# Attention and sparse feed-forward on one core: weight operands made on DVE once and stored, P1 seeded into P2's bank, steps of the attention part reordered

## The chip, the cores and the metric

The kernel runs on one NeuronCore of a Trainium2 chip. The metric is device time of one execution in microseconds (us), lower is better. The engines are TensorE (PE, with PEld for its weight loads), VectorE (DVE), ScalarE (ACT), GpSimd (POOL) and SyncE (SP), which here only issues DMAs.

## The reference

The input x is 2048 x 512. It is layer-normalised, xn = layernorm(x), and the result is x + attention(xn) + ffn(xn):

```
x_norm = layernorm(xn) * gamma + beta
q, k, v = x_norm @ qkv            # 512 x 512 each, one head, causal
attention = softmax(q k^T / sqrt(512)) v @ o_proj + xn
h = silu(xn @ w_gate) * (xn @ w_up)          # 2048 wide
ffn = keep_2_of_4(h) @ w_down                # of every 4, the 2 largest in magnitude
```

Everything is float32.

## The kernel before, in words

**Precision.** Each float32 operand is split into a part rounded to fp32r (hi) and the rest (lo), and each product is three matmuls: hi hi, hi lo, lo hi. ACT makes the hi parts (a cast), and DVE or POOL the lo parts (a subtraction). The three matmuls are lines 511 to 513 in attention, 635 to 637 for gate and up, 712 to 714 for down.

**Attention** (lines 66 to 102, 114 to 126, and the loops over `steps`). The 2048 rows are 4 chunks of 512, or 16 tiles of 128. q and k are folded into one matrix (mu), v and o_proj into another (vo). For each chunk there are statistics (`stat`, `x_stats`, `x_rstd`, `x_scale`), a way of turning them into rows (`row_turn`, `row_store`, `row_spread`; for chunk 0 `x_rows` and `x_turn`), xh (the normalised, transposed x: `xh_pre` on DVE, an affine step and the hi part on ACT, the lo part on DVE), `z` (mu times xh) and `v` (one product for each tile), and `xn`, the transposed layernorm of x, which is stored to DRAM (`xn_store`) for the feed-forward part. For each tile i there are `scores`, `exp`, `head` (PE turns the first two groups of 4 key tiles), and `attend` (the other turns and the products with v). The order is written out by hand in the list `steps`: what stands in `before`, `between` and `beside` is put in front of head i, behind it, and between scores i+1 and attend i. Every engine runs the same list in order and does its own part of each step, with semaphores between the engines, so an engine that waits in one step holds back all that it has in later ones. PE's products share 4 banks, its turns 3.

In the kernel before, POOL does these steps: `x_rstd`, the lo part of the last weight splits (line 479), `xn` (lines 487 and 490), and the weight sums and lo parts (lines 446 to 456).

**Feed-forward** (from line 630). The rows are worked in two passes of 1024, and each pass in 8 sets of 256 hidden units for each of the 4 positions in a group of 4; N_Q = 16 sets, n = 0 to 15. Gate and up of a set are each a 2 x 2 block product, done with 7 products by Strassen's scheme in Winograd's form: P1 to P7, on operands A11, A12, A22 and the sums S1 to S4 of the weights, and B11, B21, B22 and T1 to T4 of x. `block_product` is 6 matmuls, so a set has 14 x 6 = 84. PE's order is P1, P2, P6, P7, P5, P3, P4, gate and up in turn, in banks 0 and 1 (X), 2 and 3 (Y), 4 and 5 (Z). P1, P1+P6, P1+P6+P5 grow in X; ACT copies each stage to SBUF (`snapshot`, line 827). P2 is made in Y by itself, and DVE adds the copy of P1 to it (`add_sum` with fill F_P2); P7 and P4 are in Z and DVE adds copies to them (`add_sum`, line 1066). ACT applies silu, DVE multiplies by up (`hidden`, line 1072).

Then the 2 of 4 are picked for half a set, i = n - 2: ACT makes magnitudes (line 831), DVE compares them (`first_beats`, `last_beats`), counts (`count_beats`), zeroes (`keep`), ACT and DVE split the result (`kept_hi`, `kept_lo`), and PE multiplies by w_down (`down`: 48 matmuls in 4 tiles that alternate between banks 6 and 7; a tile needs the bank that `add_down`, line 1082, of two tiles ago set free). PE's order is gate_up(n), down(n-2), gate_up(n+1).

The waits that matter here: P4 of gate waits for the sum of P7 (`summed`), as it is added to the same bank; P2 waits only for DVE's sum of the set before; P6 waits for the copy of P1.

For each of the 16 sets, 1 MB of weights is loaded (`load_set`), POOL makes S1 to S4 (lines 446 to 451, in two halves), ACT the hi parts (line 745, 4 x 896 columns) and POOL the lo parts (line 455), though the second pass uses the same weights. There are two operand buffers, `wset[0]` and `wset[1]`. The down weights of two halves (1 MB) are loaded, split by ACT (`down_hi`) and POOL (`down_lo`) for every second set. Between the passes, X's operands are made again for the other 1024 rows (`X_first` to `X_fourth`, `X_lo_half` on DVE, `X_halves` on ACT); they are seven pairs of hi and lo.

Of the kernel before, what the change touches and what calls it, by code (L numbers as in the profile page):

```python
# [26 lines left out]
def attention_ffn(nc, x, x_t, qkv_t, o_proj, gamma, beta, w_units, w_down, out):  # L27
# [45 lines left out]
    between = {3: [z[1][1], row_turn[2], row_store[2], *z[1][2:4], row_spread[2]],  # L73
               7: z[2],
               11: z[3]}
    beside = {0: [v[0][1], *stat[2][2:4], x_stats[2], x_rstd[2], xt_load[2]],
              1: [xh_pre[1][0], v[0][2], xh_pre[1][1]],
              2: [*xh[1], v[0][3], x_scale[2], xn_store[0]],
              3: [*xn[1], stat[3][0], stat[3][1]],
              4: [v[1][0], stat[3][2], stat[3][3], x_stats[3], x_rstd[3], xt_load[3]],  # L80
              5: [v[1][1], *xh_pre[2], x_scale[3], xn_store[1]],
              6: [v[1][2], row_turn[3], row_store[3], *xh[2], row_spread[3]],
              7: [v[1][3], *xn[2]],
              8: [xn_store[2], v[2][0]],
              9: [v[2][1], *xh_pre[3]],
              10: [v[2][2], *xh[3], *xn[3]],
              11: [v[2][3], xn_store[3]],
              12: [*v[3], ("w_load", 0, 0)],
              13: [("w_sum", 0, 0), ("w_sum", 0, 1), ("w_hi", 0, 0), ("w_hi", 0, 1), ("w_lo", 0, 0), ("w_lo", 0, 1)],
              14: [("w_hi", 0, 2), ("w_hi", 0, 3), ("w_lo", 0, 2), ("w_lo", 0, 3)]}  # L90
# [38 lines left out]
    with ExitStack() as ctx:  # L129
# [36 lines left out]
        beats_a, beats_b = at("beats_a", 56 * KB, [P, 2, W], BF16), at("beats_b", 58 * KB, [P, 2, W], BF16)  # L166
        beats_c, pair_sum = at("beats_c", 60 * KB, [P, 2, W], BF16), at("pair_sum", 62 * KB, [P, 2, W], BF16)
# [4 lines left out]
        wsum_early = [at(f"wsum_early{m}", o * KB, [P, 2, NOP, P], F32) for m, o in enumerate((56, 168))]  # L172
        acc = at("acc", 96 * KB, [P, 2 * TC, D], F32)
        dw = at("dw", 112 * KB, [P, 2, 2, 2, D], F32R)
        dw_last = at("dw_last", 0, [P, 2, 2, 2, D], F32R)
        dw_raw, dw_last_raw = at("dw_raw", 112 * KB, [P, 2, 2, 2, D], F32), at("dw_last_raw", 0, [P, 2, 2, 2, D], F32)
        g_sum = [at(f"g_sum{i}", (160 + 2 * i) * KB, [P, W], F32) for i in range(4)]
# [4 lines left out]
        last_mag = [at(f"last_mag{i}", o * KB, [P, G, W], F32) for i, o in enumerate((128, 64))]  # L182
        last_hi = [at(f"last_hi{i}", (o + 8) * KB, [P, G, W], F32R) for i, o in enumerate((128, 64))]
        last_lo = [[at(f"last_lo{i}_{r}", (o + 16 + 2 * r) * KB, [P, W], F32R) for r in range(G)] for i, o in enumerate((128, 64))]
# [1062 lines left out]
```

## Time and profile before

| | |
|---|---|
| median of 3 runs | 963.36 us (962.62 to 967.53) |
| the profiled execution | 965.22 us |
| its span, first to last instruction | 963.4 us |
| instructions | 9777 |
| mean granted clock of TensorE | 0.940 of full speed |
| PE busy | 850.4 us (88%) |
| DVE busy | 637.4 us (66%) |
| ACT busy | 342.1 us (36%) |
| POOL busy | 350.0 us (36%) |
| DMA | 66.72 MB, mean 69 GB/s |

Matmul rows overlap: one shows 0.39 us from start to end at full clock, though the next starts 0.23 us after it. The lists of groups and of single instructions name an engine, a line, and tiles as out<-in. "Idle before" is how long the engine had stood still, and behind the arrow what ended it. Times in the trace count from the first instruction; attention ends and the first feed-forward set begins at 374.0, set 2 at 412.1, set 15 at 900.3.

### The profile page before, as it was taken

Reading aid. Unit: us, or ns where it says so; the run is one execution under the profiler, and the core shown is the slowest. Engines: PE = TensorE matmul, PEld = TensorE weight load, DVE = VectorE, ACT = ScalarE, POOL = GpSimd, SP = SyncE. Lnnn points to the kernel's source line nnn. Section 1 sums busy time; section 2 is a strip of 40 time slices with the busy share of each in tenths; the row PEclk is TensorE's granted clock in tenths of the full one; section 3 lists DMA queues with packets and bytes.
Section 4 is the critical chain, followed back from the end, with each engine's and each line's share of the span. In section 5 each row is a group of like instructions: output and inputs, shape, how many; then the busy total and the mean of one; then the engine's idle time right before and its main releaser. Section 6 shows DMA issues by size and latency. Waiting matters only on the chain. (4 is left out here: it accounts for less than half of the span.)

```text
span 963.4 us, 9777 instructions
## 1 busy us (share of the span) xinstructions
PE 850.4 (88%) x3635; PEld 690.3 (72%) x3635; DVE 637.4 (66%) x919; ACT 342.1 (36%) x546; POOL 350.0 (36%) x259
## 2 busy tenths in 40 slices
PE   7796898989999998988898898887898988988987
PEld 5575776777778887867686686676776776866875
DVE  6846474235323346396966966999769769669597
ACT  5413214113212325443443443454434334434341
POOL 2324031003002232674464455455625724734120
PEclk9987999999999999998898998897988988998999
DMA  9323233001001132211011021221034020120102
GB/s 339 119 76 111 77 110 121 22 22 66 23 23 55 33 142 97 100 44 45 25 64 44 3 85 44 88 88 55 33 113 150 1 87 13 32 72 17 45 0 88
DMA packets 32319, 66.72 MB, mean 69 GB/s; under 512 B 3168, under 2 KB 3216, under 8 KB 31888
## 3 DMA queue, kind: packets, MB, share of 16 engines
q1 hardware_dynamic: 28096, 58.50, 18.1%
q10 hardware_dynamic: 4176, 7.60, 2.3%
q8 instruction: 29, 0.48, 0.2%
q14 instruction: 18, 0.15, 0.1%
HBM read 53.48 MB, written 12.61 MB: 69 GB/s over the span
## 5 line engine op out<-in xcount | busy, mean ns | idle before, releaser
L635 PE MATMUL bank<-X_hi,wset 128*128 128x512 f32 x448 | 189.4, 423 | 62.8 <-DVE g_sum L1066 58.9
L455 POOL TENSOR_TENSOR wset<-wsum,wset 128x896 fp32r<-128x896 f32 x60 | 140.5, 2368 | 175.3 <-ACT wset L745 175.3
L636 PE MATMUL bank<-X_lo,wset 128*128 128x512 f32 x448 | 186.0, 415 | 0.0
L637 PE MATMUL bank<-X_hi,wset 128*128 128x512 f32 x448 | 185.7, 415 | 0.0
L635 PEld LDWEIGHTS bank<-X_hi,wset 128*128 128x128 f32 x448 | 91.3, 204 | 88.4 <-DVE g_sum L1066 59.8
L637 PEld LDWEIGHTS bank<-X_hi,wset 128*128 128x128 f32 x448 | 91.1, 203 | 20.3
L636 PEld LDWEIGHTS bank<-X_lo,wset 128*128 128x128 f32 x448 | 91.9, 205 | 19.1
L1082 DVE TENSOR_TENSOR acc<-bank,acc 128x512 f32<-128x512 f32 x64 | 43.4, 689 | 83.8 <-PE bank L714 83.8
L712 PE MATMUL bank<-dw,hs_hi 128*128 128x512 f32 x224 | 88.4, 395 | 0.0
L713 PE MATMUL bank<-dw,hs_hi 128*128 128x512 f32 x224 | 87.8, 392 | 0.0
L714 PE MATMUL bank<-dw,hs_lo 128*128 128x512 f32 x224 | 87.3, 390 | 0.0
L446 POOL TENSOR_TENSOR wsum<-wsum 128x256 f32<-128x256 f32 x30 | 24.0, 801 | 163.6 <-DMA wsum<-w_units 163.6
L511 PE MATMUL bank<-v_hi,pT_hi 128*128 128x512 f32 x136 | 55.6, 409 | 11.0 <-issue 7.4
L511 PE MATMUL bank<-xT_hi,zg_hi 128*128 128x512 f32 (+3 forms) x160 | 59.2, 370 | 5.6 <-DVE zg_lo L1011 5.6
L513 PE MATMUL bank<-xT_hi,zg_lo 128*128 128x512 f32 (+3 forms) x160 | 58.1, 363 | 0.0
L512 PE MATMUL bank<-xT_lo,zg_hi 128*128 128x512 f32 (+3 forms) x160 | 58.0, 362 | 0.0
L1023 DVE TENSOR_SCALAR_CACHE_REDUCE raw<-bank 128x512 f32<-128x512 f32 (+3 forms) x36 | 21.5, 600 | 54.0 <-PE bank L513 54.0
L745 ACT CAST wset<-wsum 128x896 fp32r<-128x896 f32 x60 | 53.3, 938 | 4.5 <-POOL wsum L451 4.5
L513 PE MATMUL bank<-v_hi,pT_lo 128*128 128x512 f32 x136 | 53.8, 395 | 0.0
L512 PE MATMUL bank<-v_lo,pT_hi 128*128 128x512 f32 x136 | 53.6, 394 | 0.0
L487 POOL TENSOR_TENSOR xt_raw<-xt_raw,spread 128x1024 f32<-128x1024 f32 x8 | 19.5, 2434 | 90.7 <-DVE xh_raw L993 90.7
L739 ACT CAST pT_hi<-bank 128x512 fp32r<-128x512 f32 (+3 forms) x40 | 19.6, 524 | 87.2 <-PE bank L553 42.9
(164 smaller groups left out, 1755.2 us busy)
## 6 DMA issues: line engine op xcount, KB each, us to landing
wsum<-w_units SPq DMA_DIRECT2D x60, 256.0 KB, 3.7
dw_raw<-L_ffn_w_down SPq DMA_DIRECT2D x14, 512.0 KB, 4.7
xw<-L_attn_x SPq DMA_DIRECT2D x4, 1024.0 KB, 9.3
xt_raw<-x_t SPq DMA_DIRECT2D x8, 512.0 KB, 7.0
xn_t<-xt_raw SPq DMA_DIRECT2D x8, 512.0 KB, 7.4
X_raw<-xn_t SPq DMA_DIRECT2D x8, 512.0 KB, 4.2
acc<-resid SPq DMA_DIRECT2D x2, 2048.0 KB, 9.3
result<-acc SPq DMA_DIRECT2D x16, 256.0 KB, 2.3
```

What stands on the lines that cost most here:

```text
L455: nc.gpsimd.tensor_tensor(wset[q % 2][:, m, 1, :, :], sums_at(q, m), wset[q % 2][:, m, 0, :, :].bitcast(F32), ALU.subtract).then_inc(w_op_ ...
L511: pe.matmul(dst, l_hi, r_hi, start=(n == 0 and flags.get("first", True)), stop=False)
L512: pe.matmul(dst, l_hi, r_lo, start=False, stop=False)
L513: last = pe.matmul(dst, l_lo, r_hi, start=False, stop=(n == len(pairs) - 1 and flags.get("last", True)))
L635: pe.matmul(dst[:], u[:, 0, :], x_hi, start=(first and kt == 0), stop=False, skip_group_check=True)
L636: pe.matmul(dst[:], u[:, 0, :], x_lo, start=False, stop=False, skip_group_check=True)
L637: last = pe.matmul(dst[:], u[:, 1, :], x_hi, start=False, stop=(kt == 1), skip_group_check=True)
L712: pe.matmul(dst, s_hi, d_h, start=(r == 0), stop=False)
L713: pe.matmul(dst, s_hi, d_l, start=False, stop=False)
L714: last = pe.matmul(dst, s_lo, d_h, start=False, stop=(r == G - 1))
L745: nc.scalar.copy(wset[q % 2][:, m, 0, :, :], sums_at(q, m)).then_inc(w_hi, 1)
L1082: nc.vector.tensor_tensor(acc[:, tile, :], down_bank(i, t)[:], acc[:, tile, :], ALU.add).then_inc(added, 1)
```

## The change

It does these things:

- The sums, the lo parts of the weight operands, the lo parts of the down weights, the last lo parts of the v/o splits and xn are issued on DVE. POOL keeps only `x_rstd` and the constants. The sums are one group of four operations of 512 columns for each set, where they were two groups of 256.
- The operands of sets 0 to 7 are stored to a DRAM tensor as they are made (3.67 MB each, `store_set`), and sets 8 to 15 load them from there (`load_made`), with no sums, hi or lo parts.
- ACT copies P1 from banks 0 and 1 to banks 2 and 3, and P2 is accumulated on top of it; ACT applies silu to bank 2 itself, and DVE multiplies by bank 3 (`first_hidden`). The two DVE adds of P1 to P2 go. P2 waits for the copies.
- Each v product is a tile ahead of where it was, and v of a new chunk stands behind its z. The rows of chunk 0 are turned ahead of the first two v/o weight products. xn, xh and statistics steps stand at other tiles.
- In tile 15 ACT makes two X halves ahead of its probabilities, not four, and DVE makes the X sums behind them.
- Some buffers have other places; the last down weights are loaded a little later.

```diff
+    wop_dram = nc.dram_tensor("w_operands", (NQ, P, 4 * 2 * NOP * P), F32, kind="Internal").ap()
...
-              xw_load[2], xt_load[1], split[2][2], split[3][2], split[2][3], split[3][3], x_scale[0], ("x_rows", 0, 0), vo[0], vo[1],
-              ("x_turn", 0, 0), *xh_pre[0], vo[2], xh[0][0], stat[1][0], xh[0][1], stat[1][1], vo[3], xh[0][2], stat[1][2], xh[0][3],
-              stat[1][3], x_stats[1], x_rstd[1], *xn[0], xw_load[3], *z[0][0:2], x_scale[1], z[0][2], row_turn[1], row_store[1], z[0][3],
-              ("scores", 0, 0), row_spread[1], exp[0], v[0][0], *stat[2][0:2]]
+              xw_load[2], xt_load[1], split[2][2], split[3][2], x_scale[0], ("x_rows", 0, 0), split[2][3], split[3][3],
+              ("x_turn", 0, 0), vo[0], vo[1], *xh_pre[0], vo[2], xh[0][0], stat[1][0], xh[0][1], stat[1][1], vo[3], xh[0][2], stat[1][2],
+              xh[0][3], stat[1][3], x_stats[1], x_rstd[1], xw_load[3], *z[0][0:2], x_scale[1], z[0][2], row_turn[1], row_store[1],
+              z[0][3], row_spread[1], ("scores", 0, 0), exp[0], v[0][0], xn[0][0], v[0][1], xn[0][1], xn_store[0]]
     before = {3: [z[1][0]]}
...
+    between = {3: [z[1][1], x_scale[2], *z[1][2:4], v[1][0]],
+               7: [*z[2], v[2][0]],
+               11: [*z[3], v[3][0]]}
+    beside = {0: [v[0][2], xh_pre[1][0]],
+              1: [xh_pre[1][1], v[0][3], *xh[1][0:2]],
+              2: [*xh[1][2:4], *stat[2], x_stats[2], x_rstd[2], xt_load[2]],
+              3: [v[1][1], *stat[3], x_stats[3], x_rstd[3], xt_load[3]],
+              4: [v[1][2], row_turn[2], row_store[2], *xn[1], row_spread[2], xn_store[1], x_scale[3]],
+              5: [v[1][3], *xh_pre[2]],
+              6: [row_turn[3], row_store[3], *xh[2], row_spread[3], *xn[2], xn_store[2]],
+              8: [v[2][1]],
+              9: [v[2][2], *xh_pre[3]],
+              10: [v[2][3], *xh[3], *xn[3], xn_store[3]],
+              11: [v[3][1]],
+              12: [*v[3][2:4], ("w_load", 0, 0)],
+              13: [("w_sum", 0, 0), *fills("w_hi", 0)],
+              14: fills("w_lo", 0)}
...
+            def flat(q):
+                return wset[q % 2][:].bitcast(F32).rearrange("p m h o i -> p (m h o i)")
+            def store_set(q):
+                sp.wait_ge(w_op_ready, 4 * q + 4)
+                sp.dma_start(wop_dram[q], flat(q)).then_inc(set_stored[q % 2], 16)
+            def load_made(n):
+                q = n % NQ
+                sp.wait_ge(set_stored[q % 2], 16 * (q // 2 + 1))
+                sp.dma_start(flat(n), wop_dram[q]).then_inc(set_loaded[n % 2], 16)
...
                 if n + 2 < N_Q:
                     sp.wait_ge(full[1], FILLS * (n + 1))
-                    load_set(n + 2)
+                    if n + 2 < NQ:
+                        sp.wait_ge(set_stored[n % 2], 16 * (n // 2 + 1))
+                        load_set(n + 2)
+                    else:
+                        load_made(n + 2)
+                if n + 1 < NQ:
+                    store_set(n + 1)
...
                 X_wait(1)
                 for m in range(2):
-                    if n:
-                        pe.wait_ge(summed[m], 3 * (n - 1) + 1)
-                    block_product(m, n, A12, B21, Y[m], True)
+                    pe.wait_ge(kept[m], 3 * n + 1)
+                    block_product(m, n, A12, B21, Y[m], False)
...
-                snapshot(0, n, F_P1, bank[0], g_sum[0], 4 * (n - 1) + 1 if n else 0, 0)
-                snapshot(1, n, F_P1, bank[1], a_tile(n, 0), 0, a_free(n))
-                act.wait_ge(summed[0], 3 * n + 1)
-                nc.scalar.activation(g_sum[0][:], g_sum[0][:], ACT.Silu).then_inc(silu_ready, 1)
+                snapshot(0, n, F_P1, bank[0], bank[2], 4 * (n - 1) + 1 if n else 0, 0)
+                snapshot(1, n, F_P1, bank[1], bank[3], 0, 0)
+                act.wait_ge(full[0], FILLS * n + F_P2)
+                nc.scalar.activation(g_sum[0][:], bank[2][:], ACT.Silu).then_inc(silu_ready, 1)
+                early = n == 0 or 3 <= n < NQ - 1
+                if early:
                     operands_hi(n + 1, 0)
                     operands_hi(n + 1, 1)
...
+                if early or n == 1:
+                    for m in range(2 if early else 0, 4):
+                        operands_hi(n + 1, m)
+                if n >= 4 and n % 2 == 0:
                     down_hi(n // 2 - 1)
+                elif n == N_Q - 1:
+                    down_hi(ND // 2 - 1)
...
+                if n == 1:
+                    down_hi(0)
+                elif n == 2:
+                    for m in range(4):
+                        operands_hi(n + 1, m)
...
                     if n == NT - 1:
-                        for i in range(NOP):
+                        X_first(0)
+                        X_second(0)
+                        X_third(0)
+                        X_fourth(0)
+                        dve.wait_ge(X_summed, 4)
+                        for i in range(4):
+                            X_lo_half(0, i)
+                        sums(1)
+                        for i in range(4, NOP):
                             X_lo_half(0, i)
...
                 if picks:
                     first_beats(i)
-                add_sum(0, n, bank[2], F_P2, g_sum[0], 1)
-                add_sum(1, n, bank[3], F_P2, a_tile(n, 0), 1)
-                if picks:
                     last_beats(i)
-                hidden(n, 1, 1, g_sum[0], a_tile(n, 0))
+                first_hidden(n)
                 if picks:
                     count_beats(i)
                     keep(i, 0)
                     keep(i, 1)
+                if n == 0:
+                    operands_lo(1, 0)
+                    operands_lo(1, 1)
+                elif n <= 2:
+                    sums(n + 1)
+                if n == 1:
+                    for m in range(4):
+                        operands_lo(2, m)
+                if n >= 4 and n % 2 == 0:
+                    down_lo(n // 2 - 1)
+                elif n == N_Q - 1:
+                    down_lo(ND // 2 - 1)
                 add_sum(0, n, bank[4], F_P7, g_sum[2], 3)
...
+                elif picks and n < NQ - 1:
+                    operands_lo(n + 1, 0)
+                    operands_lo(n + 1, 1)
+                    add_down(i, 0)
+                    operands_lo(n + 1, 2)
+                    operands_lo(n + 1, 3)
+                    add_down(i, 1)
+                    add_down(i, 2)
+                    if n + 2 < NQ:
+                        sums(n + 2)
+                    add_down(i, 3)
```

## Rows read from the trace of the kernel before

**Rows 1.** The page, busy tenths of POOL in 40 equal slices of the span.
```profile
POOL 2324031003002232674464455455625724734120
```

**Rows 2.** PE's waits: line waited for, us in total, times, longest.
```profile
PE bank L635 <- DVE g_sum L1066: 58.9, 13, 7.1
PE bank L635 <- ACT g_sum L827: 3.9, 2, 3.5
PE bank L712 <- issue: 2.7, 1, 2.7
PE bank L712 <- DVE last_lo L1117: 2.6, 3, 2.2
...
PE bank L511 <- issue: 15.2, 5, 7.8
PE bank L553 <- issue: 5.8, 4, 1.4
PE bank L511 <- DVE zg_lo L1011: 5.6, 4, 1.4
...
PE bank L543 <- DVE row_stat L976: 4.9, 1, 4.9
PE bank L511 <- DVE pT_lo L916: 3.7, 3, 3.0
```

**Rows 3.** Stretches: length, busy PE, PEld, DVE, ACT, POOL (x), PEclk, DMA share, GB/s.
```profile
45.00:105.00 60.00, 46.55 (x192) 37.22 (x193) 33.49 (x72) 14.46 (x29) 20.09 (x13) 0.83 0.27 92
...
374.00:412.10 38.10, 38.10 (x170) 31.56 (x169) 16.25 (x21) 19.54 (x29) 23.81 (x16) 1.00 0.34 118
412.10:900.30 488.20, 425.44 (x1718) 344.58 (x1717) 384.21 (x441) 196.14 (x308) 243.40 (x171) 0.91 0.17 54
```

**Rows 4.** Timeline of set 6, from 563.06: start us, length us, engine, line.
```profile
563.26 2.20 ACT L831 ACTIVATE mag<-hid_a 128x512 f32<-128x512 f32 x4 [8.58 <-PE bank L714]
565.36 0.56 ACT L827 COPY g_sum<-bank 128x512 f32<-128x512 f32 x1
...
570.03 5.08 POOL L455 TENSOR_TENSOR wset<-wsum,wset 128x896 fp32r<-128x896 f32 x2 [8.04 <-ACT wset L745]
...
570.51 2.62 DVE L1072 TENSOR_TENSOR hid_a<-g_sum,hid_a 128x512 f32<-128x512 f32 x1
573.05 2.61 DVE L1098 TENSOR_TENSOR pair_sum<-beats_b,beats_c 128x1024 bf16<-128x1024 bf16 x1
...
583.43 0.68 DVE L1066 TENSOR_TENSOR g_sum<-bank,g_sum 128x512 f32<-128x512 f32 x1
...
584.17 0.80 PE L635 MATMUL bank<-X_hi,wset 128*128 128x512 f32 x1 [4.62 <-DVE g_sum L1066]
```

**Rows 5.** Timeline of DVE in set 15, with POOL idle.
```profile
908.33 0.69 DVE L1098 TENSOR_TENSOR pair_sum<-beats_b,beats_c 128x1024 bf16<-128x1024 bf16 x1
909.05 0.42 DVE L1100 TENSOR_TENSOR beats_b<-beats_b,beats_c 128x512 bf16<-128x512 bf16 x1
```

**Rows 6.** Groups by form: busy us, mean ns of one, idle before.
```profile
L745 ACT CAST wset<-wsum 128x896 fp32r<-128x896 f32 x60 | 53.3, 938 | 4.5 <-POOL wsum L451 4.5
...
L1087 DVE TENSOR_TENSOR beats_a<-mag 128x1024 bf16<-128x1024 f32 x14 | 17.1, 1224 | 19.6 <-ACT mag L831 19.6
```

**Rows 7.** Timeline in attention: row scale, splits of chunk 1, a turn, a split.
```profile
42.55 2.30 DVE L969 SCALAR_TENSOR_TENSOR row_stat<-mean_var,row_stat 128x4 f32<-128x4 f32 x1 [1.41 <-POOL rstd L476]
...
81.34 6.54 DVE L1002 TENSOR_TENSOR xT_lo<-xh_raw,xT_hi 128x512 fp32r<-128x512 f32 x4 [2.24 <-ACT xT_hi L781]
...
236.47 0.52 PE L553 MATMUL bank<-ident,raw 128*128 128x128 f32 x3 [1.45 <-issue]
...
241.16 0.69 DVE L1002 TENSOR_TENSOR xT_lo<-xh_raw,xT_hi 128x512 fp32r<-128x512 f32 x1 [0.68 <-ACT xT_hi L781]
```

**Rows 8.** DMA: a stretch with a full queue (columns as rows 3), and an issue.
```profile
10.00:28.00 18.00, 17.23 (x80) 13.91 (x79) 15.36 (x31) 7.67 (x14) 6.04 (x8) 1.00 1.06 387
...
xw<-L_attn_x SPq DMA_DIRECT2D x4, 1024.0 KB, 9.3
```

More of the change, by code:

```diff
@@ L180, in attention_ffn @@
         hs_lo = [at(f"hs_lo{r}", o * KB, [P, W], F32R) for r, o in enumerate((156, 158, 92, 94))]
-        last_mag = [at(f"last_mag{i}", o * KB, [P, G, W], F32) for i, o in enumerate((128, 64))]
-        last_hi = [at(f"last_hi{i}", (o + 8) * KB, [P, G, W], F32R) for i, o in enumerate((128, 64))]
-        last_lo = [[at(f"last_lo{i}_{r}", (o + 16 + 2 * r) * KB, [P, W], F32R) for r in range(G)] for i, o in enumerate((128, 64))]
+        last_at = ((0, 8, 32), (64, 72, 80))
+        last_mag = [at(f"last_mag{i}", o[0] * KB, [P, G, W], F32) for i, o in enumerate(last_at)]
+        last_hi = [at(f"last_hi{i}", o[1] * KB, [P, G, W], F32R) for i, o in enumerate(last_at)]
+        last_lo = [[at(f"last_lo{i}_{r}", (o[2] + 2 * r) * KB, [P, W], F32R) for r in range(G)] for i, o in enumerate(last_at)]
         hid_a = [at(f"hid_a{i}", (176 + 2 * i) * KB, [P, W], F32) for i in range(6)]
@@ L689, in bank_free @@
                 elif i == ND - 3:
-                    pe.wait_ge(summed[t - 2], 3 * last + 1)
+                    if t == 2:
+                        pe.wait_ge(silu_ready, 4 * last + 1)
+                    else:
+                        pe.wait_ge(hid_ready, 4 * last + 1)
                 elif i == ND - 2:
@@ L696, in bank_free @@
                     else:
-                        pe.wait_ge(summed[t - 2], 3 * last + 3)
+                        pe.wait_ge(summed[t - 2], 2 * last + 2)
                 else:
@@ L806, in _ @@
                     if n == NT - 1:
-                        X_halves(0, range(4))
+                        X_halves(0, range(2))
                 elif kind == "attend":
@@ L949, in _ @@
             for kind, n, k in steps:
-                if kind == "split" and not pool_splits(n, k):
+                if kind == "split":
                     dve.wait_ge(w_hi_ready[n], k + 1)
@@ L993, in _ @@
                     nc.vector.tensor_tensor(part, part, row_over(n, 3), ALU.add).then_inc(xh_scaled, 1)
+                elif kind == "xn":
+                    t = xt_raw[n][k]
+                    if n == 0:
+                        dve.wait_ge(rows_kept, 2)
+                    done = step(nc.vector.tensor_tensor(t[:], t[:], row_over(n, 0), ALU.mult))
+                    dve.wait_ge(vec_step, done)
+                    nc.vector.tensor_tensor(t[:], t[:], row_over(n, 1), ALU.add).then_inc(xn_ready[n], 1)
+                elif kind == "w_sum":
+                    sums(n)
+                elif kind == "w_lo":
+                    operands_lo(n, k)
                 elif kind == "row_turn":
@@ L1066, in add_sum, with first_hidden @@
                 nc.vector.tensor_tensor(dst[:], src[:], dst[:], ALU.add).then_inc(summed[m], 1)
+            def first_hidden(n):
+                dve.wait_ge(silu_ready, 4 * n + 1)
+                dve.wait_ge(full[1], FILLS * n + F_P2)
+                if a_free(n):
+                    dve.wait_ge(hs_ready, a_free(n))
+                nc.vector.tensor_tensor(a_tile(n, 0)[:], g_sum[0][:], bank[3][:], ALU.mult).then_inc(hid_ready, 1)
             def hidden(n, result, sums, silu, up):
@@ L1070, in hidden @@
                 if sums:
-                    dve.wait_ge(summed[1], 3 * n + sums)
+                    dve.wait_ge(summed[1], 2 * n + sums)
                 nc.vector.tensor_tensor(up[:], silu[:], up[:], ALU.mult).then_inc(hid_ready, 1)
@@ L1123, in last_block @@
                 add_sum(1, n, bank[5], F_P4, a_tile(n, 1), 3)
-                hidden(n, 4, 3, g_sum[1], a_tile(n, 1))
+                hidden(n, 4, 2, g_sum[1], a_tile(n, 1))
             for n in range(N_Q):
@@ L1146, in _ @@
                     kept_lo(i, 1)
-                hidden(n, 2, 2, g_sum[2], b_tile(n, 1))
+                hidden(n, 2, 1, g_sum[2], b_tile(n, 1))
                 if picks:
@@ L1159, in _ @@
                     last_block(n)
+                if n == 1:
+                    down_lo(0)
                 if n == NQ - 1:
```

161 lines of the change are left out of this document (51 added, 110 removed).

## The prediction

> **What bounds the kernel now.** I read the busy tenths first: TensorE (PE) is the busiest engine, and POOL is at work a third of the time and more from attention's end on [rows 1]. Then who holds PE up: 58.9 us go to one wait, 13 times, on the vector engine's sum in line 1066 [rows 2]. Then the stretches. Sets 0 and 1 of the feed-forward part take 38.1 us for 168 matmuls with no stall and clock 1.00, so a matmul is worth 0.2268 us and a full set (84 gate/up and 48 down matmuls) 29.9 us; yet the 13 sets from 412.1 to 900.3 take 488.2 us where 13 x 29.9 = 389 would do, at clock 0.91 [rows 3]. Of these 99 us, 62 are PE's waits for sums and copies [rows 2]; the other 37, 2.8 a set, are matmuls at the lower clock level (1.2 GHz) after each wait: the first one after it takes 0.80 us [rows 4].
>
> The timeline of set 6 says why the sum is late. DVE's product of silu and up, its pair sum and its counts take 2.5 to 2.6 us each, and run side by side with four POOL operations of that same length; the sum of P7 then starts at 583.43, and PE, which needed it for P4 at 579.5, has lost 4.6 us [rows 4]. At 908 to 909, with POOL idle, the same operations take 0.69 and 0.42 us [rows 5]. So a POOL operation with operands in SBUF holds back a DVE operation with two SBUF inputs for its whole length; those that read PSUM stay at 0.68 [rows 4]. In attention it is the same: 2.30 us for a 4-column operation at 42.55, in front of PE's 4.9 us wait, and 6.54 us for four splits at 81.34, in front of PE's 7.8 us wait [rows 2, 7].
>
> **Feed-forward, the part that goes.** All large POOL work goes. In a set DVE loses one product at 2.62 to 0.69, a pair sum at 2.61 to 0.69 and two counts at 2.5 to 0.42: 8 us, and two g_sum adds of 0.68 (P2 now adds itself). Counted from the set's start, DVE then has keep 0 and 1 behind it at about 11, while the copy of P5 it also needs comes at 13.2; in even sets the two down_lo (1.2 each by the 1024-column row [rows 6]) end at 14.2. P7's sum is done at 14.8 at the latest and PE wants it at 16.5. The wait goes in all 13 sets, and with it the lower clock: 99 us.
>
> **What it adds.** (a) P2 starts only when P1 was copied. ACT comes to that copy behind four magnitudes, 2.20 us, and needs 0.56 [rows 4]: ready at 2.9 of the set, against PE at 2.72. The trace has no copy from PSUM to PSUM. From below it is the copy from PSUM to SBUF, 0.56 [rows 4], from above twice that. I take the row, whose source and size are the same: 0.2 us in each of 13 sets, 2.6; at double length it would be 0.9 a set, 9 more in all. The Trainium skill (ScalarE: Activation LUTs, Step-by-step: what each stage is for) says ScalarE writes PSUM sooner than SBUF; by that the sum would lose at most the 2.6; no row here shows such a write.
> (b) Operands on DVE, sets 2 to 6: sums 4 x 0.69 = 2.7; four lo of 896 columns between 0.69 (512) and 1.22 (1024), 1.09 each and 1.04 apart: 4.2. A set's other DVE work, at its undisturbed pace, is two comparisons of 1024 columns at 1.14, the counts with the pair sum at 3.0, and 22 operations of 512 columns that follow one another every 0.6: 18.5, so it has 25.4, or 27.8 in even sets, of 29.9. Two lo stand in front of add_down 0, which frees the bank for PE's third down tile: DVE is through at 25.1, PE wants it at 24.7. 0.45 in four sets, 1.0 in set 2, where ACT makes the hi halves last: 2.8.
> (c) Set 8: without POOL the second X pass is faster on DVE (X_lo 1.2 each), but P2 now waits for ACT, whose four last X halves (1.05 each) run to 32.2 from set 7's start, then magnitudes and the copy: 34.9 against 32.8. 2.1 us, and DVE a bit late behind it: 2.3.
> (d) Second pass: DVE and ACT have no operand work. What must arrive is one 3.67 MB load a set, issued when a gate/up ends and needed 41 us later. With the queue full the engines move 387 GB/s [rows 8]: 9.5 us, hidden. Stores of 3.67 MB in the first pass stand before the next down weights in the same queue: issued at 27.6 of set 3 they end at 8 of set 4, the weights land at 10 and 11.5, ACT comes for them at 10.8. Nothing, but with 0.3 us to spare; at half that rate the store ends 9 later and it is up to 9 us in sets 4 and 6 each.
> (e) The end: last_mag's first comparison no longer sits beside POOL, and down_hi is off ACT's path there: PE's wait of 2.7 and its clock go, the 2.2 us wait on last_lo stays [rows 2]: 63.1 becomes 58.8.
> (f) SP's waits: in the first pass it waits for the store of a buffer's last set before it loads the next one (stored nearly a set before), then for DVE's last lo of the following set (27.6) before it stores that; behind it stand only the down weights, which wait for down's end at 30.5 anyway, and, in sets 8 and 9, result stores with the second pass's acc load behind them: that load is issued at some 33 of set 9 and used at 22 of set 10. Moved buffers cost nothing, except that dw_last may be loaded only when set 14's products are done, 19 us into it, for ACT at 9 of set 15. In set 1 the sums of set 2 wait for its load; in the trace its second half is summed 6.7 us after the set's start, where DVE now comes for it at 6.5: 0.2 us, before a P7 sum with 2 us of room.
> Sum: 38.2 + 389 + 2.6 + 2.8 + 2.3 + 58.8 = 493.7 us, for 589.4 now.
>
> **Attention, 374 us now.** SP's row store and spread for chunks 2 and 3 stay ahead of the xn stores and of the xh steps that need them by a tile. Up to 105: the x_scale in front of the row turn shrinks to 0.5, -3.9; z of chunk 1 waits 5.9 instead of 8.2 (xn's four DVE steps of 1.25 delay tile 2 by 2.5, the splits come sooner), -2.3; the 1.4 wait of scores behind z goes, since v stands between, -1.4. The clock there, 0.83 over 60 us [rows 3], is 20 us at the lower level, some 6 of them idle, so it costs 7; I leave 2, -5. The rows' turn now stands before the first v/o weight products, and PE idles from 19.4 to 23.1: +3.6. Together -9.
> From 105 on: seven waits of 1.45 (the one at 236.47 stands for them) [rows 2, 7] and one of 3.0 for the split of a just made v go, as v is a tile ahead: -13.2; two waits behind z, -2.8; the wait of 3.0 in tile 15 goes, ACT has two X halves there and not four, with its clock -4.7 [rows 2].
> New are waits for in-order work. Tile 10: v, then four ACT/DVE splits 1.38 apart, end 9.5 us after the scores (241.16 + 0.69), as now; two xn of 2.5 follow on DVE and only then pT_lo of the third key group: 15.1, where PE wants it at 8.5: +6.6, and 2.5 of clock. Tile 13: sums on DVE, then four hi parts of 0.94 on ACT [rows 6] before its pT_hi: +3.2. Tile 7: v no longer covers chunk 2's splits, z waits 2.5. Tiles 9 and 14: 1.1. Together +15.9.
> 374 - 9 - 20.7 + 15.9 = 360.2.
>
> **The sum.** 360.2 + 493.7 = 853.9 of span; the profiled execution was 1.8 us over its span (965.2), so 855.7, and it stood 1.9 above the median of the runs (963.4). Forecast: 854 us, against 963.4.
>
> **The rivals.**
> The copy from PSUM to PSUM is long, or ACT comes late to it, so that PE stalls at every P2: 16 x 0.9, 868. For it: no row shows such a copy. Chance 0.10.
> Attention gives back what it gains (xn and sums stand in DVE's order in front of pT_lo in more tiles than I traced): 374, so 868. 0.07.
> DVE is the bound of the first pass. Against: 2 us of slack in each set by the steps above. For: the order is fixed, and one late load of weights (d) goes into the next set. Then sets 2 to 7 keep a wait like now, 4.4 and 2.8 us of clock: +43, 897. 0.10.
> The edit removes no stall, because the 2.6 us rows were slow by themselves: then DVE gets 7 us a set more and it ends near 975. The 0.42 us rows of the same shapes speak against it [rows 5]. 0.01.
> Slower than before: the SP queue becomes the bound. It now carries 3.67 + 1 + 0.5 MB in each first-pass set and 3.67 + 0.5 MB in each second-pass set, 75 MB in place of some 25; the sets wait when that takes longer than they do. At 387 GB/s it is 194 us of 494. The 1 MB xw loads took 9.3 us from issue to landing [rows 8], 113 GB/s: at that rate 75 MB need 664 us, and the kernel about 1025. It decides below 128 GB/s (75 MB in the 589 us of now). 0.03.
> A measurement of this kernel can tell about 0.5%, 5 us, from no change. The forecast has the rest, 0.69.
>
> **The numbers.** The forecast's own range is 836 to 880 (clock fully back and no new wait in attention at the low end, 16 below; the 9 us of (a) and the 18 of (d) at the high end). It takes in the first two rivals; for 8 in 10 the range reaches to most of the DVE case: 836 to 892. Faster by over 0.5%: 0.69 + 0.10 + 0.07 + 0.10 less a little for mishaps not named = 0.95. Within: 0.01. Slower: 0.04.
>
> **What would show it.** PE's wait on line 1066's successor is gone or under 5 us in total, DVE has no row over 1.3 us for 512 columns, and the mean clock is near 0.98. The sets from 2 to 14 are 30 to 31 us apart. P2 starts 0.1 to 0.3 us after P1 ends. In tile 10 PE waits some 6 us for pT_lo, at 19.4 some 3.7 us for the rows. The 3.67 MB loads and stores take 9 to 12 us each. It is wrong if PE waits at P4 in the first pass, if it waits at a set's start in the second (the load), or if DVE's long rows stay with POOL idle.

## The result and the profile after

The changed kernel takes 877.5 us (median of 4 runs, 875.8 to 878.3) against 963.0 before (962.5 to 967.5): ratio 0.910, 95% interval 0.907 to 0.913. That is inside the predicted range, on the predicted side, and 23 us above the point forecast of 854. The profiled execution took 875.8 us with a span of 874.0.

The page says that PE's busy share rose from 88% to 94%, and POOL's busy time fell from 350.0 us to 13.7.

```profile
PE 825.3 (94%) x3635; PEld 672.0 (77%) x3635; DVE 578.8 (66%) x985; ACT 314.1 (36%) x514; POOL 13.7 (2%) x33
...
PEclk9898999999899999999999999999999999999998
```

PE's waits. The first line of [rows 2], 58.9 us for the sum of P7, has no successor at all; nothing waits at P4 any more. What remains is spread over many small ones, most of them in attention.

```profile
PE bank L473 <- DVE pT_lo L887: 12.6, 5, 6.3
PE bank L473 <- issue: 6.0, 2, 3.3
PE bank L473 <- DVE xT_lo L946: 5.5, 1, 5.5
PE bank L597 <- DVE X_lo L919: 4.4, 1, 4.4
PE bank L548 <- DVE rows_wide L974: 4.0, 1, 4.0
PE bank L597 <- ACT bank L794: 3.7, 2, 1.9
PE bank L679 <- DVE last_lo L1132: 3.3, 4, 2.7
```

The stretches, with the columns of [rows 3]: attention in three parts, sets 0 and 1, sets 2 to 14, and the end.

```profile
0.00:45.00 45.00, 33.49 (x131) 27.06 (x132) 29.58 (x57) 21.59 (x35) 5.23 (x17) 0.92 0.62 222
45.00:105.00 60.00, 52.19 (x229) 41.28 (x227) 34.42 (x80) 16.87 (x33) 5.33 (x11) 0.91 0.27 93
105.00:369.20 264.20, 246.31 (x1167) 204.11 (x1166) 125.13 (x263) 64.51 (x104) 3.14 (x6) 0.98 0.22 78
...
369.20:410.20 41.00, 40.98 (x169) 33.52 (x170) 29.72 (x37) 22.04 (x33) 0.00 (x0) 0.94 0.52 199
410.20:812.40 402.20, 397.23 (x1717) 322.85 (x1716) 310.01 (x469) 167.80 (x276) 0.00 (x0) 0.99 0.46 175
...
812.40:874.00 61.60, 55.08 (x229) 43.13 (x228) 49.90 (x80) 21.31 (x36) 0.00 (x0) 0.96 0.09 35
```

The 13 sets from 2 to 14 took 488.2 us at clock 0.91; they now take 402.2 at 0.99. The first feed-forward matmul starts at 369.2, where it started at 374.0. So the feed-forward part gave 84.6 us of span and attention 4.8.

The timeline of set 6 (from 536.3): ACT's two copies of P1, and DVE. It answers to [rows 4].

```profile
538.62 1.19 ACT L794 COPY bank<-bank 128x512 f32<-128x512 f32 x2
...
542.37 0.69 DVE L1081 TENSOR_TENSOR hid_a<-g_sum,bank 128x512 f32<-128x512 f32 x1
542.97 0.68 DVE L1113 TENSOR_TENSOR pair_sum<-beats_b,beats_c 128x1024 bf16<-128x1024 bf16 x1
543.69 0.42 DVE L1115 TENSOR_TENSOR beats_b<-beats_b,beats_c 128x512 bf16<-128x512 bf16 x1
...
548.28 2.36 DVE L910 TENSOR_TENSOR dw<-dw_raw,dw 128x1024 fp32r<-128x1024 f32 x2 [1.03 <-ACT dw L717]
550.55 0.68 DVE L1073 TENSOR_TENSOR g_sum<-bank,g_sum 128x512 f32<-128x512 f32 x1
```

The pair sum and the counts have the durations that they had beside an idle POOL in [rows 5], and the product of silu and up, which now reads a bank, takes 0.69 us. P7's sum starts 14.2 us after the set's start, where it was 20.4; PE wants it at 16.5.

The DMA issues that are new took what was expected, and no set waits for one:

```profile
w_operands<-wset SPq DMA_DIRECT2D x8, 3584.0 KB, 12.0
wset<-w_operands SPq DMA_DIRECT2D x8, 3584.0 KB, 11.6
```

Two waits in the profile have a cause that the prediction did not name. The first is behind DVE's order in tile 15:

```profile
356.87 0.69 DVE L887 TENSOR_TENSOR pT_lo<-bank,pT_hi 128x512 fp32r<-128x512 f32 x1 [3.12 <-ACT pT_hi L706]
360.08 0.69 DVE L887 TENSOR_TENSOR pT_lo<-bank,pT_hi 128x512 fp32r<-128x512 f32 x1 [2.52 <-ACT pT_hi L706]
361.88 0.55 DVE L1051 TENSOR_SCALAR rows<-rows,one_rstd,neg_mean_rstd 128x512 f32<-128x512 f32 x1 [1.10 <-DMA rows<-L_attn_x]
362.34 2.55 DVE L914 TENSOR_TENSOR X_raw<-X_raw,X_raw 128x1024 f32<-128x1024 f32 x2
365.34 2.36 DVE L914 TENSOR_TENSOR X_raw<-X_raw,X_raw 128x1024 f32<-128x1024 f32 x2 [0.46 <-DVE X_raw L914]
367.74 4.63 DVE L919 TENSOR_TENSOR X_lo<-X_raw,X_hi 128x1024 fp32r<-128x1024 f32 x4
```

DVE stands idle for 3.1 and 2.5 us between the turned groups, then waits for the last row tile, and only then makes the X sums: PE stands for 4.4 us ahead of set 0. The second is ACT at the start of set 2, with the matmul that waits for it:

```profile
410.16 1.99 ACT L717 CAST dw<-dw_raw 128x1024 fp32r<-128x1024 f32 x2
412.05 2.19 ACT L798 ACTIVATE mag<-hid_a 128x512 f32<-128x512 f32 x4
414.14 1.05 ACT L794 COPY bank<-bank 128x512 f32<-128x512 f32 x2
...
414.77 0.50 PE L597 MATMUL bank<-X_hi,wset 128*128 128x512 f32 x1 [1.83 <-ACT bank L794]
```

### The profile page after: what moved, and what is told of

It reads as the page before. It is cut to its first block and busy times, and to the rows that moved or that the text cites. A ratio compares the mean times of both kernels' runs of the same rounds, so it can differ in the third digit from the quotient of the medians.

```text
span 874.0 us, 9524 instructions
## 1 busy us (share of the span) xinstructions
PE 825.3 (94%) x3635; PEld 672.0 (77%) x3635; DVE 578.8 (66%) x985; ACT 314.1 (36%) x514; POOL 13.7 (2%) x33
## 5 line engine op out<-in xcount | busy, mean ns | idle before, releaser
L597 PE MATMUL bank<-X_hi,wset 128*128 128x512 f32 x448 | 178.5, 398 | 8.7 <-DVE X_lo L919 4.4
L599 PE MATMUL bank<-X_hi,wset 128*128 128x512 f32 x448 | 176.6, 394 | 0.0
L598 PE MATMUL bank<-X_lo,wset 128*128 128x512 f32 x448 | 176.6, 394 | 0.0
L597 PEld LDWEIGHTS bank<-X_hi,wset 128*128 128x128 f32 x448 | 85.5, 191 | 32.8 <-ACT bank L794 7.9
L599 PEld LDWEIGHTS bank<-X_hi,wset 128*128 128x128 f32 x448 | 85.4, 191 | 18.2
L598 PEld LDWEIGHTS bank<-X_lo,wset 128*128 128x128 f32 x448 | 85.6, 191 | 17.4
L473 PE MATMUL bank<-xT_hi,zg_hi 128*128 128x512 f32 (+3 forms) x160 | 58.9, 368 | 1.4 <-DVE zg_lo L1016 1.4
L679 PEld LDWEIGHTS bank<-dw,hs_hi 128*128 128x128 f32 x224 | 42.0, 188 | 11.5 <-DVE acc L1097 2.9
L681 PEld LDWEIGHTS bank<-dw,hs_lo 128*128 128x128 f32 x224 | 42.1, 188 | 8.8
L680 PEld LDWEIGHTS bank<-dw,hs_hi 128*128 128x128 f32 x224 | 42.0, 188 | 8.5
L473 PEld LDWEIGHTS bank<-v_hi,pT_hi 128*128 128x128 f32 x136 | 26.4, 194 | 21.1 <-DVE pT_lo L887 12.0
## 6 DMA issues: line engine op xcount, KB each, us to landing
wset<-w_operands SPq DMA_DIRECT2D x8, 3584.0 KB, 11.6
```

What stands on the lines that cost most here:

```text
L473: pe.matmul(dst, l_hi, r_hi, start=(n == 0 and flags.get("first", True)), stop=False)
L597: pe.matmul(dst[:], u[:, 0, :], x_hi, start=(first and kt == 0), stop=False, skip_group_check=True)
L598: pe.matmul(dst[:], u[:, 0, :], x_lo, start=False, stop=False, skip_group_check=True)
L599: last = pe.matmul(dst[:], u[:, 1, :], x_hi, start=False, stop=(kt == 1), skip_group_check=True)
L679: pe.matmul(dst, s_hi, d_h, start=(r == 0), stop=False)
L680: pe.matmul(dst, s_hi, d_l, start=False, stop=False)
```

## The experiments

Two questions: which part of the change gave the 85 us, and where the 23 us are that the forecast had and the run did not.

**Seed alone, on the kernel before.** POOL keeps its work.

```diff
-                snapshot(0, n, F_P1, bank[0], g_sum[0], ...)
-                snapshot(1, n, F_P1, bank[1], a_tile(n, 0), ...)
+                snapshot(0, n, F_P1, bank[0], bank[2], ...)
+                snapshot(1, n, F_P1, bank[1], bank[3], 0, 0)
...
-                    block_product(m, n, A12, B21, Y[m], True)
+                    block_product(m, n, A12, B21, Y[m], False)
...
-                add_sum(0, n, bank[2], F_P2, g_sum[0], 1)
-                add_sum(1, n, bank[3], F_P2, a_tile(n, 0), 1)
...
-                hidden(n, 1, 1, g_sum[0], a_tile(n, 0))
+                first_hidden(n)
```

> The kernel before, with P1 copied into P2's bank by ACT and the two adds of P1 to P2 gone; POOL keeps all its work. Contention theory (the gain is the end of POOL's work beside DVE's): the long DVE rows stay at 2.5 to 2.6 us, DVE is only 2 x 0.68 = 1.4 us a set earlier, so each of the 13 waits at P4 shrinks from about 4.5 to about 3.1 and the 2.8 us of lower clock behind it stays; a wait of 0.3 to 0.5 us at P2 is new. 963 - 13 x 1.4 + 5 = 950 us (942 to 958). Rival (the seed takes P1's sum out of the chain and that frees the sets): the waits at P4 fall under 1 us and the time to 880 or less.

927.1 us (ratio to before 0.962, 0.960 to 0.964), between what the theory and the rival gave. The timeline of DVE in its set 5 (from 515.9) shows what the expectation had missed:

```profile
521.98 0.69 DVE L1075 TENSOR_TENSOR hid_a<-g_sum,bank 128x512 f32<-128x512 f32 x1
522.59 2.16 DVE L1107 TENSOR_TENSOR pair_sum<-beats_b,beats_c 128x1024 bf16<-128x1024 bf16 x1
524.78 2.24 DVE L1109 TENSOR_TENSOR beats_b<-beats_b,beats_c 128x512 bf16<-128x512 bf16 x1
526.94 2.33 DVE L1110 TENSOR_TENSOR beats_b<-beats_b,beats_c 128x512 bf16<-128x512 bf16 x1
529.31 2.23 DVE L1112 TENSOR_TENSOR pair_sum<-pair_sum,beats_a 128x512 bf16<-128x512 bf16 x1
531.46 0.41 DVE L1113 TENSOR_TENSOR pair_sum<-pair_sum,beats_a 128x512 bf16<-128x512 bf16 x1
```

Four rows of DVE are still held to 2.2 us beside four POOL lo parts, so contention is there, as expected. But with P1 seeded, the product of silu and up reads a PSUM bank and not two SBUF tiles, and it takes 0.69 us while POOL works. So the seed spares DVE the two adds and a little of the hold as well. P7's sum starts 17.9 us after the set's start, where in set 5 of the kernel before it was 19.8: 1.4 us of these 2.0 are the adds, and 0.6 is the hold, since a count takes the place of the product beside POOL and four rows are still held. Outside sets 2 and 8, PE stands still at P4 for 1.8 to 2.7 us, where it was 4.1 to 4.6 before. And behind waits that short the lower clock came only in some sets: over sets 2 to 14 the clock is 0.97, for 0.91 before, and that is the larger part of what the expectation missed. The row of sets 2 to 14, and the stretches of gate and up in set 3 and in set 5 of this run, where waits of 1.77 and 1.76 us show both cases (clock 0.93 and 1.00):

```profile
410.00:860.00 450.00, 410.61 (x1717) 326.93 (x1716) 363.80 (x415) 197.24 (x308) 241.96 (x170) 0.97 0.18 59
...
447.50:470.50 23.00, 21.18 (x85) 16.73 (x84) 21.13 (x24) 13.01 (x21) 11.81 (x8) 0.93 0.00 0
...
515.90:537.40 21.50, 19.69 (x86) 15.63 (x86) 19.57 (x21) 12.47 (x21) 11.64 (x8) 1.00 0.00 0
```

**The seed taken out of the changed kernel** (the reverse of the edit above).

> The changed kernel without the seed: P2 made by itself, and DVE adds the copies of P1 to it again. Contention theory: DVE has 1.4 us a set more to do, in front of the sum of P7, which had about 2 us to spare; so no wait over 1.5 us comes at P4, and the waits at P2 (0.34 a set, 1.8 in set 2, 1.9 in set 8) go. 872 to 880 us. Rival (the seed carries the gain): 3 to 5 us at P4 and the lower clock return in each set from 2 to 14, 940 us or more.

874.9 us (0.907, 0.904 to 0.909): within what the contention theory gave, and a little under the changed kernel. Two waits are at P4, 0.6 us in set 2 and 2.5 in set 8, where none over 1.5 was expected; in the eleven other sets from 2 to 14 there is none. With P2 by itself the second-pass sets are 29.92 us apart, exactly 132 matmuls at full clock; with the seed they are 30.26. In a kernel without POOL's work the seed brings nothing that shows. The four times together:

| | POOL's work on POOL | on DVE, stored for pass 2 |
|---|---|---|
| P2 alone, two adds | 963 | 875 |
| P2 on a seed of P1 | 927 | 877.5 |

(the right column also has the changed attention part, worth about 5, which no run has by itself). The two gains don't add: both shorten the same DVE chain ahead of P7's sum, and in the changed kernel that sum already starts 2.3 us before PE wants it (14.2 for 16.5).

**No store: the second pass makes its operands again, on DVE.**

```diff
-                    if n + 2 < NQ:
-                        sp.wait_ge(set_stored[n % 2], 16 * (n // 2 + 1))
-                        load_set(n + 2)
-                    else:
-                        load_made(n + 2)
-                if n + 1 < NQ:
-                    store_set(n + 1)
+                    load_set(n + 2)
...
-                early = n == 0 or 3 <= n < NQ - 1
+                early = n == 0 or 3 <= n < N_Q - 1
```

(with `operands_lo` and `sums` issued on DVE in sets 7 to 14 as in 3 to 6)

> The changed kernel without stores and loads of made operands: DVE and ACT make sums, hi and lo parts in the second pass too, as in sets 3 to 7; no w_operands traffic. If contention with POOL was all, DVE has room for them: sets 9 to 14 are 30.7 us apart as sets 3 to 7 are, where they were 30.3, and set 8 starts a few us later as two sets' operand work meets the X work in set 7: 882 us (879 to 892). Rival (what counts is that the second pass has less work): the waits at P4 return in the second pass, 7 x 7.2 = 50 us, 925 or more.

881.1 us (0.914, 0.912 to 0.915). Sets 9 to 14 are 30.7 us apart, 0.43 more each, and sets 7 and 8 take 7.3 us more together; sets 0 to 2 are 2.9 shorter and the end 1.3, with less lower clock there. The longest wait at P4 is 1.3 us. In the sets that the edit touches, storing 29 MB and loading it again is worth some 10 us (7.3 and 6 x 0.43); the difference between the two times is 3.6, as less lower clock in other stretches gives back 4 in this run, by no mechanism that was found.

**A dose of POOL work in the second pass**, which nothing waits for.

```diff
+            for n in range(9, 14):
+                pool.wait_ge(full[0], FILLS * n + F_P1)
+                for _ in range(8):
+                    if n in (9, 10):
+                        small_step(nc.gpsimd.tensor_tensor(scratch[:], X_hi[6][:, 0, :].bitcast(F32), X_hi[6][:, 1, :].bitcast(F32), ALU.add))
+                    elif n == 12:
+                        small_step(nc.gpsimd.tensor_copy(scratch[:], X_hi[6][:, 0, :].bitcast(F32)))
+                    else:
+                        small_step(nc.gpsimd.memset(scratch[:], 0.0))
```

> The changed kernel, with eight POOL operations of 128x512 f32 on a scratch tile added in each of sets 9 to 13, from the end of P1: in sets 9 and 10 an add with two SBUF inputs, in 11 and 13 a memset, in 12 a copy with one SBUF input. Nothing waits for them. Contention theory: beside the adds, DVE's product of silu and up, its pair sum and counts are stretched to the length of a POOL add (over 1.2 us, from 0.69 and 0.42), the sum of P7 comes 4 to 6 us later and PE waits 2 to 4 us at P4 in sets 9 and 10, with the lower clock behind it: +8 to +14 us. If only operand reads hold DVE, sets 11 and 13 are as in the changed kernel; if writes do too, they wait as well. Rival (DVE's long rows had to do with its own work): no DVE row grows, 877 us.

885.6 us (one run), and a wait of 1.8 us at P4 in set 9 (2 to 4 was expected) and of 4.1 in set 10; none in 11, 12 and 13. POOL's timeline in sets 10, 11 and 12, and under it one form of DVE (a comparison of two SBUF tiles, 128x512) in the same three sets, and in set 10 the product that reads a bank:

```profile
665.84 13.72 POOL L474 TENSOR_TENSOR scratch<-X_hi 128x512 f32<-128x512 f32 x8 [18.91 <-PE bank L610]
703.19 4.61 POOL L478 MEMSET scratch<- 128x512 f32 x8 [23.63 <-PE bank L610]
733.82 8.45 POOL L476 COPY scratch<-X_hi 128x512 f32<-128x512 f32 x8 [26.03 <-PE bank L610]
...
670.37 1.77 DVE L1118 TENSOR_TENSOR beats_c<-mag 128x512 bf16<-128x512 f32 x1
706.25 0.69 DVE L1118 TENSOR_TENSOR beats_c<-mag 128x512 bf16<-128x512 f32 x1
736.99 1.09 DVE L1118 TENSOR_TENSOR beats_c<-mag 128x512 bf16<-128x512 f32 x1
...
673.76 0.67 DVE L1092 TENSOR_TENSOR hid_a<-g_sum,bank 128x512 f32<-128x512 f32 x1
```

A POOL add lasts 13.72 / 8 = 1.72 us and the DVE row beside it 1.77; a POOL copy lasts 1.06 and DVE's row 1.09; beside memsets of 0.58 the row stays at 0.69. So in these rows a DVE operation with two SBUF inputs lasts as long as the POOL operation beside it if that one reads SBUF, be it one tile or two, and is not held by one that only writes. The rest of set 10 is held less evenly: the pair sum takes 1.18 us there and three counts 1.40 to 1.51, for 0.69 and 0.42 beside an idle POOL. The product of g_sum with a PSUM bank isn't held: 0.67 beside the adds. The Trainium skill (SBUF — State Buffer, Who interferes with whom) describes just this, a lock for the whole instruction between GpSimd operations that read SBUF and DVE operations with two SBUF inputs; the runs agree, with these numbers.

**The weight work back on POOL in the first pass** (sets 2 to 7; stores, seed and second pass unchanged).

```diff
+            for q in range(2, NQ):
+                pool.wait_ge(w_op_ready, 4 * q)
+                sums(q)
+                for m in range(4):
+                    operands_lo(q, m)
```

(`sums` and `operands_lo` on POOL, taken out of DVE's loop)

> The changed kernel, with the sums and lo parts of the weights of sets 2 to 7 back on POOL (stores, seed and second pass unchanged). Contention theory: sets 3 to 7 look as in the run with the seed alone, with DVE rows of 2.2 us or more and 2 to 3 us waits at P4: 2 to 4.5 us more for each, less 0.4 of down waits that go, so +8 to +18 us in sets 2 to 7, and sets 9 to 14 stay 30.26 us apart: 885 to 895 us. Rival (operand work on DVE is a load that POOL would spare it): sets 3 to 7 become 0.4 us faster, 875 us.

894.5 us (one run), 17 more. Waits at P4 of 4.6, 4.0, 1.8 and 4.0 us are back in sets 3 to 6, with DVE rows of 2.1 to 2.3 us, and sets 9 to 14 stay 30.26 us apart. The time is as expected, though three of the four waits are longer than the 2 to 3 us that were written down, and set 7, in which no operands are made, has none.

Then the missing 23 us.

**X sums in DVE's idle time.**

```diff
                 elif kind == "attend":
+                    if n == NT - 1:
+                        X_first(0)
+                        X_second(0)
                     for g in groups_of(kind, n):
                         probs_lo(n, g)
+                        if n == NT - 1 and g == HEAD:
+                            X_third(0)
+                            X_fourth(0)
+                    if n == NT - 1:
+                        X_lo_half(0, 0)
+                        X_lo_half(0, 1)
                     dve.wait_ge(rows_loaded[slot], 16 * (n // 2 + 1))
...
-                        X_first(0)
-                        X_second(0)
-                        X_third(0)
-                        X_fourth(0)
```

> The changed kernel, with tile 15's X sums and the first two X lo parts issued on DVE in its idle time between the last turns, ahead of the scale of the last rows (whose load lands at 361.9). If their place was the cause, PE's wait of 4.4 us before set 0 and the 2.7 us of lower clock behind it go: 871 us (869 to 874). Rival (X's loads are late themselves, or ACT's X halves are): the wait stays above 2 us, and the time within 3 us of the changed kernel's.

866.9 us (0.900, 0.897 to 0.902), 2 under the expected range. The X sums now run at 354.2 and 358.1:

```profile
354.22 2.54 DVE L914 TENSOR_TENSOR X_raw<-X_raw,X_raw 128x1024 f32<-128x1024 f32 x2
357.47 0.69 DVE L887 TENSOR_TENSOR pT_lo<-bank,pT_hi 128x512 fp32r<-128x512 f32 x1 [0.70 <-ACT pT_hi L706]
358.07 2.35 DVE L914 TENSOR_TENSOR X_raw<-X_raw,X_raw 128x1024 f32<-128x1024 f32 x2
```

PE's wait ahead of set 0 is gone, set 0 starts 4.0 us earlier and sets 0 to 2 are 2.7 us shorter. The edit accounts for 6.7 us. Another 1.0 is in sets 3 to 14, where no lower clock followed set 8's wait in this run (its row there has clock 1.00, for 0.92 in the changed kernel), and 0.8 in the end; the last 2 of the 10.6 stand in the medians and not in the two profiled executions.

**P1's copies ahead of magnitudes.**

```diff
+                    mags_first = 0 if n in (2, NQ) else 2
                     for r in range(G):
+                        if r == mags_first:
+                            snapshot(0, n, F_P1, bank[0], bank[2], 4 * (n - 1) + 1, 0)
+                            if not r:
+                                snapshot(1, n, F_P1, bank[1], bank[3], 0, 0)
                         ...
                         magnitude(i, r)
```

> The changed kernel, with ACT's copy of P1 of gate put between the second and third magnitude, and in sets 2 and 8 both copies ahead of all four. P2's waits go: 13 x 0.34 = 4.4 us, and in sets 2 and 8 2.0 of wait and 1.6 of clock each: 877 - 11 = 866 us (864 to 871; the upper end because in sets 2 and 8 the comparisons start 2 to 3 us later on DVE and P7's sum may be late by 1 to 2 us). Rival (DVE is so full in the first pass that the later magnitudes come back as a wait at P4 in even sets): 872 or more.

870.7 us (0.903, 0.900 to 0.905), at the upper end of what was expected. All waits at P2 are gone and ordinary sets are 0.34 us shorter, but in sets 2 and 8 P7's sum now comes 0.8 and 2.2 us late, as the comparisons start later on DVE, and down of set 2 waits 1.6 us: set 8 gains nothing.

**xn of chunk 3 behind head 11.**

```diff
-               11: [*z[3], v[3][0]]}
+               11: [*xn[3], xn_store[3], *z[3], v[3][0]]}
...
-              10: [v[2][3], *xh[3], *xn[3], xn_store[3]],
+              10: [v[2][3], *xh[3]],
```

> The changed kernel, with xn of chunk 3 moved on DVE from tile 10, ahead of its third turned group, to behind head 11, beside chunk 3's z products. Tile 10's wait of 6.3 us becomes 1 to 2 (the four splits of xh remain) and the lower clock behind it 0 to 1: 870 us (868 to 873). Rival (in-order work only moves): z's lo parts come late behind the 5 us of xn and PE waits 3 us or more in tile 11 or 12: 875 or more.

868.6 us (0.901, 0.898 to 0.903). Tile 10's wait falls from 6.3 to 1.55 us, its lower clock goes, and nothing waits in tiles 11 and 12: z's 48 matmuls cover the 5 us of xn.

**All of it, and more moves of the same kind.**

The further moves: two xh splits of chunks 1, 2 and 3 go behind heads 2, 6 and 10, the sums and hi parts of set 0 go from tile 13 to ahead of head 14, and `add_down` goes ahead of the lo parts.

```diff
-    before = {3: [z[1][0]]}
+    before = {3: [z[1][0]], 14: [("w_sum", 0, 0), *fills("w_hi", 0)]}
+    between = {2: xh[1][2:4],
+               6: xh[2][0:2],
+               10: xh[3][0:2],
...
-              13: [("w_sum", 0, 0), *fills("w_hi", 0)],
...
+                    add_down(i, 0)
                     operands_lo(n + 1, 0)
                     operands_lo(n + 1, 1)
-                    add_down(i, 0)
+                    add_down(i, 1)
                     operands_lo(n + 1, 2)
                     operands_lo(n + 1, 3)
-                    add_down(i, 1)
```

> All three edits (X sums early, P1's copies first, xn of chunk 3 later) and, by the same rule, more steps moved off the front of a turned group that PE waits for: two xh splits of chunks 1, 2 and 3 behind heads 2, 6 and 10; the sums and hi parts of set 0 from tile 13 to ahead of head 14; in sets 3 to 6 add_down 0 ahead of the first two lo parts. If the waits are each local, the gains add: 877 - 10 - 7 - 9, as measured one by one, then 2.7 in tile 13, 2.8 in tile 7, 2.5 at z of chunk 1, 1.5 in tile 10 and 0.4 x 4 in down: 840 us (837 to 848). Rival (in-order work only moves, as it fills DVE's next idle time): half of it or less is kept, 857 or more.

843.1 us (0.874, 0.872 to 0.877), 3 over the sum of the gains: they add. It beats both kernels, the changed one by 34 us. Its stretches of sets 0 and 1, sets 2 to 14, and the end, and what PE still waits for:

```profile
345.80:384.00 38.20, 38.20 (x169) 31.39 (x169) 27.73 (x36) 19.49 (x30) 0.00 (x0) 1.00 0.57 214
384.00:777.80 393.80, 390.62 (x1718) 321.61 (x1717) 308.53 (x469) 168.80 (x276) 0.00 (x0) 1.00 0.47 179
777.80:838.50 60.70, 54.50 (x229) 43.21 (x227) 49.72 (x80) 21.35 (x36) 0.00 (x0) 0.97 0.09 35
```
```profile
PE bank L475 <- DVE xT_lo L954: 5.5, 1, 5.5
PE bank L475 <- DVE pT_lo L895: 3.6, 3, 2.5
PE bank L550 <- DVE rows_wide L982: 3.4, 1, 3.4
PE bank L681 <- DVE last_lo L1145: 3.0, 2, 2.7
PE bank L599 <- DVE g_sum L1086: 2.9, 2, 2.1
```

The 13 sets from 2 to 14 take 393.8 us, where full clock without a stall gives 389. What is left is above all the wait for the first weight splits, the rows' turn at 19, tile 2, the last comparison chain, and P4 in sets 2 and 8 (0.8 and 2.1).

## Why the prediction was right, and what it mis-sized

**The main cause was right and is shown.** The prediction blamed POOL operations with operands in SBUF for the long DVE rows, and expected all 13 waits at P4 to go with the lower clock. They went. Three runs carry it: POOL adds put back where nothing needs them bring the long rows and the waits back, the weight work put back on POOL in the first pass brings them back in that pass only, and taking out the seed or the store, which leaves POOL idle, does not. The prediction's remark that operations which read PSUM are not held came true, but not by the row that it names: at 583.43 POOL had been idle for 3 us (its last lo part ended at 580.44). The product at 0.67 to 0.69 beside a working POOL, in the run with the seed alone and in the one with the dose, is what shows it.

**The rivals.** A long PSUM-to-PSUM copy: it took 0.54 to 0.58 us, about as long as the one to SBUF. DVE as the bound of the first pass: no wait at P4 in any set. The SP queue: 3.5 MB landed in 12 us, and no set waited. Attention giving everything back: it kept 4.8 us.

**Term by term**, feed-forward 504.8 us of span against 493.7:
- (a), 0.2 us a set at P2, was 0.34: 1.5 more in the eleven sets outside 2 and 8.
- (b) left out set 2's ACT: `down_hi(0)`, 2.0 us, stands in ACT's order ahead of the magnitudes and P1's copies. Cost in set 2: 1.8 of wait, where 0.2 was taken, and 1.6 of lower clock. The steps had followed `operands_hi` of that set, and not what ACT carries into it. The down stalls themselves were 0.4 in four sets and 0.5 in set 2, 0.7 less than taken.
- (c), 2.3 at set 8, was 3.7: the wait was 1.85, for 2.1 worked out, but the lower clock behind it, 1.6, had not been counted.
- (d) held: store 12.0, load 11.6 us, for 9.5 at the full rate, and hidden.
- (e): the end took 61.6 us and not 58.8. The wait on last_lo was 2.7 (2.2 taken) and 1.6 us of lower clock stood behind it, which the sum had dropped with the other wait of 2.7; P2 of set 15, 0.3, was in no term.
- Not in the sum at all: 2.7 us of lower clock in set 0, behind the wait ahead of it.

Attention ended at 369.2, for 360.2. Two steps failed. One is that on tile 15, where the prediction let its wait go since ACT has two X halves there and not four. That wait did go; but the same line of the change puts DVE's X sums behind the last pT_lo and behind the load of the last row tile. That is 4.4 us, and it was never followed. The other is the clock up to 105, of which 5 of the 7 us were to come back. They did not: the clock there was 0.92 and 0.91, so some 17 us were at the lower level, 3 of them idle, and it cost 7 again, behind the rows' turn at 19, chunk 0's z at 37 and the waits at 77 and 83. Less large are that wait of chunk 0's z itself, 2.0, the lower clock behind tile 13's wait, 1.7, and tile 7, 0.8 (3.3 for 2.5). Together these are 14 us; 5 came out better elsewhere, in part as the wait for the row scale went whole (4.9 for 3.9 taken), chunk 1's z waited 5.2 for 5.9 and the 0.8 at 24.6 went, and in part untraced.

The waits that were taken one by one came out well: tile 10 6.3 (6.6), tile 13 2.7 (3.2), tile 2 2.5 (2.5), tile 9 0.8, the rows' turn 4.0 (3.6).

So against the 20 us of span that were missing stand about 6 of waits from two in-order placements (X sums in tile 15, `down_hi(0)` ahead of set 2), about 14 of lower clock behind waits that had been left out or costed without it (up to 105, tile 13, sets 0, 2 and 8, the end), and about 5 of small waits (z of chunk 0, P2, tile 7, last_lo), less 5 to 6 that came out better. The prediction thus had the lost clock too low in most places, and how much of it follows a wait also changes from run to run. The other 3 us are between the profiled execution and the runs: the forecast had put the median 1.9 under the profiled execution, as before, and it stood 1.7 over it. Two bounds of the range were added up wrong by little: the low end of 836 lies 18 below the forecast, and not 16, and the two terms of the high end, 9 and 18, make 881.

## What to carry to other kernels

Look for DVE rows with two SBUF inputs that take longer beside a POOL row than alone, up to the length of that row: the cure is to empty POOL, or to let DVE read one input from PSUM, and the two don't add. Price every new wait, and every wait that stays, with the lower clock that may stand behind it, by waits of that length in the same trace. And where a step is moved in an in-order engine, list what stands ahead of it and idle time just before: moving such steps to where another engine is busy for long gave 34 us here without removing any work.

## What the runs showed of the hardware that was not expected

- A POOL operation that only writes SBUF (memset, 0.58 us) leaves DVE alone (0.69), and one that reads a single tile holds it (1.09 beside 1.06).
- The lower clock behind a wait is not a function of the wait alone. In the run with the seed alone, a wait of 1.77 us in set 3 was followed by the lower clock and those of 1.76, 2.31 and 2.70 in sets 5, 6 and 7 were not; in the changed kernel and the one with X sums early, the same 1.85 us wait in set 8 was followed by the lower clock in one (0.92 over the set's gate and up) and not in the other (1.00). What decides it was not found.
- ACT's copies of 128x512 from PSUM to PSUM took 0.571 us on average in the changed kernel, and those to SBUF 0.589. The Trainium skill (ScalarE: Activation LUTs, Step-by-step: what each stage is for) says that ScalarE writes PSUM faster than SBUF; the order agrees, and at this size the difference is 0.02 us.
